# Second expert product of a mixture layer: 96-column products one chunk at a time, against rounds of four 32-column tiles over four chunks

## What is computed

```
x = x + conv_attention(layernorm_channels(x))
t = tokens(x)
n = layernorm(t)
gate = top2_normalised(softmax(n @ gate_w + gate_b))
h = gelu(einsum('bsd,edh->ebsh', n, w1) + b1, exact)      # 4 experts, 96 -> 384
y = einsum('ebsh,ehd->ebsd', h, w2) + b2                   # 384 -> 96
t = t + einsum('bse,ebsd->bsd', gate, y)
```

## Time and profile before

| what | us |
|---|---|
| median of 3 runs | 738.1 |
| lowest, highest run | 738.0, 743.66 |
| the profiled execution | 742.88 |
| its span in the trace | 741.0 |
| PE busy | 696.9 |
| DVE busy | 577.5 |
| ACT busy | 385.4 |
| POOL busy | 216.1 |

### The profile page before, as it was taken

How to read it: one execution, slowest core, us unless ns; L and a number is a source line. 1 busy time by engine, 2 the same in 40 slices (tenths; PEclk the granted TensorE clock), 3 DMA queues, 4 the chain that set the end, 5 groups by cost and what they waited for, 6 DMA issues and landing times.

```text
span 741.0 us, 9747 instructions
## 1 busy us (share of the span) xinstructions
PE 696.9 (94%) x3250; PEld 487.7 (66%) x3250; DVE 577.5 (78%) x1511; ACT 385.4 (52%) x722; POOL 216.1 (29%) x184
## 2 busy tenths in 40 slices
PE   5798998899999999899999899999998999999996
PEld 5556566566676666566766566666665665888884
DVE  4899548899999767799998277899984375677774
ACT  2313125654554626644556217544543256999995
POOL 4001700011228500111157200221285121344443
PEclk9997999799999999999999899999999999999998
DMA  9007200134565421354644522344745201121211
GB/s 191 19 0 200 55 8 1 40 70 90 99 180 118 99 48 19 69 110 102 170 120 76 95 48 47 73 86 87 206 104 109 40 25 45 47 75 48 65 47 38
DMA packets 29697, 58.71 MB, mean 79 GB/s; under 512 B 6128, under 2 KB 20176, under 8 KB 29360
## 3 DMA queue, kind: packets, MB, share of 16 engines
q0 software_dynamic: 11584, 17.90, 15.6%
q1 hardware_dynamic: 14336, 32.64, 15.2%
q10 hardware_dynamic: 3728, 7.55, 3.2%
HBM read 30.35 MB, written 14.65 MB: 61 GB/s over the span
## 4 chain that ended last, share of the span: by engine, by line
PE 62%; DMA 13%; POOL 10%; ACT 6%; DVE 5%; issue 4%; POOLq 0%; ACTq 0%
PE py L746 13%; PE pd L662 8%; POOL big L1469 8%; DMA xbuf<-ye 8%; PE ph L578 7%; PE ph L762 3%; PE ph L764 3%; PE ph L763 3%; DMA value_table<-valT 3%; PE pa L650 3%; PE pa L529 2%; PE ph L782 2%; PE ph L784 2%; PE ph L783 2%; PE py L794 2%
## 5 line engine op out<-in xcount | busy, mean ns | idle before, releaser
L746 PE MATMUL py<-hid,w 128*96 128x448 f32 x504 | 235.0, 547 | 12.3 <-ACT hid L1006 9.0
L1006 ACT ACTIVATE hid<-ph,b 128x448 f32<-128x448 f32 x252 | 159.2, 634 | 143.5 <-PE ph L764 138.9
L762 PE MATMUL ph<-x_hi,w_hi 96*128 96x448 f32 x252 | 165.2, 655 | 0.0
L1480 POOL DMA_DIRECT2D xbuf<-ye x76 | 67.6, 889 | 327.3 <-DMA xbuf<-ye 173.4
L1469 POOL DMA_INDIRECT big<-value_table,rows x64 | 85.8, 1340 | 87.0 <-DVE rows L1193 55.2
L746 PEld LDWEIGHTS py<-hid,w 128*96 128x96 f32 x504 | 81.4, 164 | 31.6 <-ACT hid L1006 13.2
L764 PE MATMUL ph<-x_hi,w_lo 96*128 96x448 f32 x252 | 93.4, 371 | 0.0
L763 PE MATMUL ph<-x_lo,w_hi 96*128 96x448 f32 x252 | 92.7, 368 | 0.0
L1416 DVE SCALAR_TENSOR_TENSOR ye<-py,b,gate_all 96x448 f32<-96x448 f32 x112 | 75.4, 675 | 11.7 <-PE py L746 6.5
L1482 POOL TENSOR_TENSOR xbuf<-xbuf,ye 96x448 f32<-96x448 f32 x36 | 54.2, 1506 | 98.9 <-DVE ye L1416 96.2
L1443 DVE TENSOR_TENSOR hid_lo<-hid,hid_hi 128x448 fp32r<-128x448 f32 x84 | 59.5, 709 | 27.8 <-ACT hid L1015 27.4
(11 more groups left out here) (165 smaller groups left out, 1052.7 us busy)
## 6 DMA issues: line engine op xcount, KB each, us to landing
gate_all<-gate_rows SPq DMA_DIRECT2D x56, 336.0 KB, 3.4
xbuf<-ye POOLq DMA_DIRECT2D x76, 168.0 KB, 3.4
value_table<-valT ACTq DMA_DIRECT2D x6, 1176.0 KB, 8.1
out<-xbuf SPq DMA_DIRECT2D x28, 168.0 KB, 2.0
xbuf<-in_x SPq DMA_DIRECT2D x3, 1176.0 KB, 10.5
value_table<-valT SPq DMA_DIRECT2D x2, 672.0 KB, 5.3
big<-value_table,rows POOLq DMA_INDIRECT x64, 2.8
value_table<-valT SPq DMA_DIRECT2D x2, 504.0 KB, 4.4
```

The lines of the kernel that those rows point to most:

```text
L746: nc.tensor.matmul(py[e % 2][0:C, 0:GPIX], w2[:, c, :], hid[:, k % 3, :], start=(j == 0), stop=(j == CPE - 1)).then_inc(hid_used, 1)
L762: nc.tensor.matmul(bank, w1_hi[:, cols], xh(b, g), start=True, stop=False)
L1006: nc.scalar.activation(hid[:, k % 3, :], ph[k % 2][:, 0:GPIX], ACT.Gelu, bias=b1[:, k % NCH:k % NCH + 1]).then_inc(hid_act, 1)
L1480: pool.dma_start(to, ye[0:C, e, :], accum_op=ALU.add).then_inc(ye_summed, 16)
```

## The change

**Second products in rounds.** Chunks are taken in fours (a quad), one of each expert, in the order 3, 0, 1, 2. PE issues four first products and then three rounds (`second_products`). Round r makes four products of 32 columns each: three are the three column blocks of one expert (0, 1 or 2) on its own chunk, and the fourth, on PSUM partitions 96 to 127, is column block r of expert 3. So 3 rounds replace 4 products of 96 columns, and `py` has three banks, one for each round. `hid` has four slots. All is plain f32; the split form for the last 84 chunks, `split_w2` and the second GELU go. The tables count steps, five to a quad (four first products and one block of rounds); by their numbers 28 of the 84 quads have a stage piece behind their first or second product.

**Outputs.** DVE makes three outputs of 128 partitions for a group in place of four of 96. Partitions 96 to 127 of each hold a third of expert 3, which POOL adds by DMAs of its own: for each group one DMA of expert 0 into x, one of expert 2 into expert 1, three of 32 rows into x, and one of the pair into x. The last group is summed by three 32-row DMAs and three additions on POOL. SP loads gates by four DMAs in place of two.

**Banks.** Stage pieces share three banks; a table gives each its bank.

**DVE.** The taps of the value convolution of the next image are cut to single blocks and spread behind the additions of y and the splits of the tokens; the masking of quarter q follows the sampling of quarter q+1.

```diff
-                def second(k):
-                    c, n = k % NCH, k // CPE
-                    e, j = n % EXPERTS, k % CPE
-                    pe.wait_ge(hid_act, k + 1)
...
-                    nc.tensor.matmul(py[e % 2][0:C, 0:GPIX], w2[:, c, :], hid[:, k % 3, :], start=(j == 0), stop=(j == CPE - 1)).then_inc(hid_used, 1)
...
                 def first_product(k):
...
+                    if k >= 2:
+                        pe.wait_ge(hid_act, k - 1)
...
+                def second_products(m):
+                    n, j = m // CPE, m % CPE
+                    start, stop = j == 0, j == CPE - 1
+                    last_chunk = chunk(QUAD * m)[2]
+                    for r in range(ROUNDS):
+                        if start:
+                            wait(pe, ye_ready, ROUNDS * (n - 1) + r + 1)
+                        pe.wait_ge(hid_act, QUAD * m + r + 2)
+                        c = chunk(QUAD * m + r + 1)[2]
+                        for i in range(BLOCKS):
+                            rows = slice(i * CB, (i + 1) * CB)
+                            nc.tensor.matmul(py[r][rows, 0:GPIX], w2[:, c, rows], hid[:, r + 1, :], start=start, stop=stop)
+                        rows = slice(r * CB, (r + 1) * CB)
+                        nc.tensor.matmul(py[r][C:128, 0:GPIX], w2[:, last_chunk, rows], hid[:, 0, :], start=start, stop=stop).then_inc(hid_used, 1)
+                def issue_to(end):
+                    while issued[0] < end:
+                        m, i = issued[0] // STEPS, issued[0] % STEPS
+                        if i < QUAD:
+                            first_product(QUAD * m + i)
+                        else:
+                            second_products(m)
+                        issued[0] += 1
...
-                    y=(74, 74, 74, 74, 74, 74, 74, 74),
+                    y=(97, 97, 97, 97, 97, 97, 97, 97),
...
+            def last_sums(step, outs, to):
+                g = BY_DMA
+                if step == 0:
+                    pool.wait_ge(ye_ready, ROUNDS * g + 1)
+                    p.tensor_tensor(to, to, outs[0:C, 0, :], ALU.add).then_inc(last_added, 1)
+                elif step < 1 + BLOCKS:
+                    i = step - 1
+                    pool.wait_ge(ye_ready, ROUNDS * (g + 1))
+                    pool.dma_start(outs[i * CB:(i + 1) * CB, 1, :], outs[C:128, i, :], accum_op=ALU.add).then_inc(last_summed, 16)
+                elif step == 1 + BLOCKS:
+                    pool.wait_ge(last_added, 1)
+                    p.tensor_tensor(to, to, outs[0:C, 2, :], ALU.add).then_inc(last_added, 1)
+                else:
+                    pool.wait_ge(last_added, 2)
+                    pool.wait_ge(last_summed, 16 * BLOCKS)
+                    p.tensor_tensor(to, to, outs[0:C, 1, :], ALU.add).then_inc(last_added, 1)
```

More of the change, by code:

```diff
@@ L62, with attended_jobs @@
 EARLY_SLOTS, VALUE_HALF = 2, 4
+GATES_AFTER = 3
 def jobs(b, name, number):
     return [(b, name, g) for g in range(number)]
[L69 to L73, removed]
+def attended_jobs(b):
+    order = []
+    for n in range(NY):
+        order += [(b, "y", n)] + ([(b, "x1T", n - 2)] if n >= 2 else [])
+    return order + [(b, "x1T", NG - 1)]
@@ L91, in dve_jobs @@
[L91 to L102, removed]
+        order += jobs(b, "valT", QT) + (jobs(b + 1, "xT", QT) if more else []) + jobs(b, "keyT", 2)
+        order += (jobs(b + 1, "pad", 2 * BLOCKS) if more else []) + jobs(b, "kv", QUARTERS) + jobs(b, "mix", QUARTERS) + attended_jobs(b)
@@ new lines, in pe_jobs, with job_table @@
+        order += (jobs(b + 1, "offT", 2) if more else []) + x1_back_jobs(b)
+        order += (jobs(b + 1, "offc", 2) + jobs(b + 1, "offs", 1)) if more else []
+    return order
+BANKS = 3
+BANKS_OF = dict(y=(2, 1), x1T=(0,), kv=(2, 1), x1c=(2, 1), gateT=(0,), offs=(2,), mix=(0, 1))
+EARLY_BANKS_OF = dict(y=(2, 3), x1T=(0, 1), kv=(2, 3, 4), mix=(0, 1), x1c=(2, 1))
+BY_DVE = ("kv", "y", "x1c", "offs")
+def job_table():
+    table, last, done = {}, [None] * (BANKS + 2), {True: 0, False: 0}
+    turns = {}
+    for job in pe_jobs():
+        b, name, g = job
+        banks = (EARLY_BANKS_OF if b == 0 and name in EARLY_BANKS_OF else BANKS_OF).get(name, (0, 1))
+        bank = banks[g % len(banks)]
+        by_dve = name in BY_DVE
+        done[by_dve] += 1
+        table[job] = bank, done[by_dve], last[bank]
+        last[bank] = by_dve, done[by_dve]
+    return table
@@ L358, in build @@
         gate_out = sem("gate_out")
-        gate_in = [sem(f"gate_in{i}") for i in range(2)]
+        gate_in = sem("gate_in")
         x_high = sem("x_high")
@@ L1118, in norm_x1, with tap @@
                 turn()
-            def tap(m, k, dst, stride, ready, blocks):
+            def tap(m, k, dst, stride, ready, blocks, ops):
                 dy, dx = k // 3, k % 3
                 order = blocks if k % 2 == 0 else blocks[::-1]
-                for i in order:
+                for i in order[ops]:
                     src = xpad[:, i, dy:dy + QH:stride, dx:dx + W:stride]
@@ L1217, in head @@
                     off_tap(k)
-                for k in range(TAPS):
-                    value_tap(b, k)
+                values_to(b, TAPS, no_turn)
                 normalise_off(b, no_turn)
@@ L1312, in rest @@
                 gates_of(b, turn)
-                split_x1(b, range(FIRST_SPLITS, NG), turn)
+                for g in range(FIRST_SPLITS, NG):
+                    split_x1(b, [g], turn)
+                    if with_head:
+                        values_to(b + 1, VALUES_BY_SPLIT[g], turn)
                 if with_head:
```

440 lines of the change are left out of this document (194 added, 246 removed), and 33 rows, old and new, of tables (OUTPUTS_AHEAD, SUMS_AHEAD).

## The result

The changed kernel takes 757.7 us (median of 4 runs, 752.8 to 759.1) against 738.1 for the kernel before: 19.6 us or 2.7% by the medians; the ratio on record is 1.0214, 95% interval [1.0164, 1.0264]. So it is slower by 2 to 3%, clear of the noise. The time lies inside the predicted range of 717 to 768, but 16 us above the 742 and above the forecast's own range of 735 to 752. The two profiled executions differ by 14.8 us of span (755.8 and 741.0); the rest of the 19.6 is that the profiled execution of before was one of its longer ones.

What follows compares the result with a forecast made beforehand. PE's instructions end to end were taken as the bound; -3.4 (quads), -1.6 (split form), +5 (taps), -3 (masks), +5 (end), +2 (ACT) sum to +4.0 on 738.1, so 742 us; own range 735 to 752, whole range 717 to 768.

Steps and rivals of the forecast that it cites:

- What bounds it: From the first expert chunk at 133.7 us on, the time is PE's instructions laid end to end.
- Rounds and quads: Expert phase: a round takes 0.75 us, a quad 5.41, or 5.04 with a stage piece; -3.4 us in all.
- The first rival: Third first product of a quad: no wait there, a quad is 5.04 us everywhere; 721 us, chance 0.23.
- the third (dearer rounds, 797): Rounds: each pass leaves a 32-column weight load uncovered at 0.11 us, 55 us more; 797 us, chance 0.12.
- Value taps: Taps among the additions of y: DVE has 0.45 us too much each time and PE waits; +5 us (0 to +8).
- split form: Last 84 chunks: the waits at its beginning and end go; -1.6 us.
- ACT's term: Evacuations of stage pieces share ACT's queue with GELU and delay it in 28 quads; +2 us (0 to +6).
- Masking: Masking behind each sampling: about three masks that PE waits for go in each image; -3 us (0 to -7).
- The end: Last group: three accumulating DMAs and an addition follow the last output; 6.3 us in place of 1.2, +5 us.
- The second rival: DVE's outputs hold PE up at the py banks, 0.7 us late over 27 groups, 19 us; 761 us, chance 0.17.
- the 8 us given as its sign: PE's waits for DVE's outputs adding up to over 8 us would show the forecast wrong.

## Why the prediction was right or wrong

**What bounds it: right.** From the first chunk on PE's instructions lie end to end; DVE is 76 us and ACT 56 us less busy over the span, and that stretch stayed at 600 us.

**Rounds and quads: right to the hundredth.** A round takes 0.75, the first tile starts 0.08 behind the last wide product (701.25 + 0.20 to 701.53; 0.09 forecast), the third first product stands at 705.52 where PE was free at 705.25 (0.27; 0.26 forecast), and the quad is 5.41. The first rival (no wait at the third product, 721 us) and the third (dearer rounds, 797) fall with it. The Trainium skill, TensorE: Matmul & The Clock Gate, section Part 3, gives a speedup of 2.38 for three column tiles; by that a round was an estimated 0.94. The trace has 0.75 with four tiles, and the measurement decides.

**Value taps: DVE's period was right, its price on PE was not there.** DVE and PE in the second image (image 1), answering to the earlier trace rows, and the stretch in which its y begins:

```profile
289.08 0.55 DVE L1347 TENSOR_TENSOR xbuf<-pa,xbuf 96x392 f32<-96x392 f32 x1
...
292.14 0.56 DVE L1347 TENSOR_TENSOR xbuf<-pa,xbuf 96x392 f32<-96x392 f32 x1
...
292.10 2.14 PE L683 MATMUL pa<-query,mix_area 128*96 128x392 f32 x6
294.85 2.14 PE L683 MATMUL pa<-query,mix_area 128*96 128x392 f32 x6
...
272.60:279.44 6.84, 6.80 (x12) 3.45 (x12) 1.65 (x4) 1.31 (x4) 2.29 (x4) 0.50 0.71 156
```

DVE's period is 3.06 us (2.76 before, 3.2 forecast), with no idle left on DVE. But PE goes on with a piece of y every 2.75 us (292.10 to 294.85), as before, and none of its waits stands at L683. With two banks the last piece (294.85) needs the addition of 292.14, which was done 2.2 us earlier: DVE falls behind by 0.3 us at each piece, and eight pieces are too few for that to reach PE. In this profile y does take 21.6 us instead of 19.4, but it begins at half clock (274.87, in the 6.8 us of the last line); with the same taps and less half clock there, in the run with the masks of image 0 put back, it takes 19.6. So the step "PE waits for it, because y has two banks" failed: the term of +5 is at most some 0.3 in this image (an estimate: 19.6 - 19.4). The two runs with the taps elsewhere show this to be the cheapest of the three places tried.

**The expert phase as a whole: the sum fits, in part by luck.** Quads, split form, taps, masks and ACT made -1 us in the prediction (-3.4, -1.6, +5, -3, +2). Measured from first chunk to PE's end: -0.5. Without the taps the same terms make -6. What filled their place was not told apart: ACT's term was not measured by itself, and the changed kernel's profile has about 25 us of half clock in this stretch where that of before has 18, which can hide some 3 us (an estimate: half of the difference).

**Masking: here the prediction failed.** It put one number, -3 (0 to -7), on "masking behind each sampling" for every image, from one PE wait of 2.97 us in image 2, with the sentence that the gathers still set the end of the sampling. In images 1 to 3 of the changed kernel the sign holds (6.8 us between two runs). In image 0 it is the other way: +8.4 us at the first chunk. The step left out is the question of what stands ahead of the awaited instruction on PE. The trace of before had the answer (DVE's first sampling and first mask of image 0, and PE's kv):

```profile
82.39 0.45 DVE L1335 TENSOR_SCALAR key_area<-big,w 98x96 f32<-98x96 f32 x2 [3.08 <-ACT keyT L866]
...
98.09 0.29 DVE L1348 TENSOR_TENSOR kv_area<-pd,head_mask 96x128 f32<-96x128 f32 x1 [1.72 <-PE pd L634]
...
97.39 2.20 PE L634 MATMUL pd<-keyT,key_area 98*32 98x128 f32 x48
```

PE's kv of image 0 comes in one block from 97.39 on, behind convolutions, and DVE's samplings begin at 82.39. A mask put between two samplings there is a new wait, and the samplings queued behind it on DVE are what PE needs next.

**The end: right in its first half, the second not seen.** Forecast +5 between last output and store; measured 5.5 - 1.2 = +4.3, since three issues took 2.36 together and a 32-row DMA landed 2.5 us from issue, not 3.4. The other +2.5 is POOL's closing time behind its last instruction, 7.6 instead of 5.1, which the prediction's sum does not have. With POOL out of the last group the end costs less than before the change: 5.2 us behind the last output instead of 6.3.

**The second rival** named 761, near the measured time, by DVE's outputs holding PE up. That is not what happened: "PE py L786 <- DVE ye L1404" adds up to 1.2 us, 6.0 more at the weight loads, together below the 8 us given as its sign and far from its 19. A right number for another reason. The range reached up to 768 for this rival, so that the measured time lies inside it is luck.

Summed up: +4.0 forecast, +14.8 in the profiles. The gap of 10.8 is the start (8.4, image 0's mask, a share of it clock), the end (6.8 instead of 5: POOL's closing, less what the DMAs fell short of their term) and 0.5 in the expert phase. The medians differ by 4.8 us more than the profiles, as the profiled execution of before was a long one.

## What to carry to other kernels

Before a step is moved between two others on one engine, look in every stage, the first one above all, at when the other engine really delivers what it waits for; a gain read from one image may be a loss in an image whose order is different. A wait between two engines that feed each other is priced by what stands behind it on the waiting engine, and a wait that leaves TensorE idle may be paid a second time in granted clock. Keep the engine with the longest closing time off the last microseconds, and lend a bank that no stage uses any longer to the loop that waits for one.

## What the runs showed of the hardware that was not expected

A round of four 32-column tiles with all 128 rows and float32 operands took 0.75 us, as long as one 96-column product had taken for one chunk: the fourth tile was free, and so were its weight loads. The time from POOL's last instruction to the end of the span was 5.1 us before and 7.6 in the changed kernel, stayed at 7.4 when POOL's last three DMAs were left out, and no longer showed where POOL ended early (2.5 us behind the last addition, with POOL done 13 us before the end). A wait of 12 us on DVE, which is not the bottleneck, put the first chunk back by 9.0 us, and some 3 of these are clock: the granted clock stood at half for 60 us of the changed kernel's span and for 42 in the profile with the mask put back (9 and 11 of them behind PE's end).
